# Delta stage of a four-stage sequence kernel: queries projected by channel and convolved on GpSimd, decay exponents read from rows in DRAM, beta as a bias of the exponential

## The reference

```
qkvz = x @ W_in                       # 128 -> 4*1024
q, k, v, z = split(qkvz)
b, a = split(x @ W_ba)                # 16 each
q, k, v = silu(conv(q, k, v))         # causal, 4 taps, one filter per channel
beta = sigmoid(b);  g = -exp(max(A_log, -2.3)) * softplus(a + dt_bias)
q = l2norm(q) * 64 ** -0.5;  k = l2norm(k)
for each position t:                  # S is 64x64 for each head
    S = S * exp(g[t])
    S = S + outer(k[t], (v[t] - k[t] @ S) * beta[t])
    o[t] = q[t] @ S
y = rmsnorm(o) * norm_w * silu(z)
out = y @ W_o
```

## Time and profile before

| | us |
|---|---|
| median of 3 runs | 7614.07 |
| lowest and highest | 7606.62 and 7653.81 |
| the profiled execution, its own time | 7602.55 |
| span of its trace | 7600.8 |

### The profile page before, as it was taken

One profiled execution on the slowest core, in us unless ns is written; L12 is line 12 of the kernel. 1 busy time (PEld: TensorE's weight loads), 2 busy tenths in 40 slices (PEclk: granted clock), 3 DMA queues, 4 the chain that ended last, 5 costly groups with the idle time before them and its releaser, 6 DMA issues. The chain is left out here.

```text
span 7600.8 us, 186089 instructions
## 1 busy us (share of the span) xinstructions
PE 6383.9 (84%) x68255; PEld 4549.0 (60%) x68256; DVE 3882.0 (51%) x7259; ACT 3145.8 (41%) x6176; POOL 1951.7 (26%) x1826
## 2 busy tenths in 40 slices
PE   2889999998999999999999999967588868887577
PEld 2566666666666666666666666646366646665477
DVE  3445545555455554555555555455444446666433
ACT  0444444444444444444444444414233325554155
POOL 2323223232232322223223232234100010001554
PEclk8999999999999999999999999979799989998588
DMA  3910000000000000000000000011100000000114
GB/s 101 322 35 1 2 1 1 1 1 2 1 1 2 1 2 1 1 1 1 2 1 1 2 1 1 1 35 50 33 0 0 0 2 0 0 0 22 36 56 117
DMA packets 92899, 160.08 MB, mean 21 GB/s; under 512 B 14156, under 2 KB 75636, under 8 KB 89588
## 3 DMA queue, kind: packets, MB, share of 16 engines
q1 hardware_dynamic: 70036, 121.89, 5.4%
q0 software_dynamic: 14080, 26.64, 1.0%
q10 hardware_dynamic: 8320, 4.19, 0.2%
HBM read 119.30 MB, written 104.06 MB: 29 GB/s over the span
## 5 line engine op out<-in xcount | busy, mean ns | idle before, releaser
L677 PE MATMUL bank<-wc,hT 128*128 128x512 f32 x3144 | 1517.6, 607 | 89.3 <-issue 83.9
L677 PEld LDWEIGHTS bank<-wc,hT 128*128 128x128 f32 x3144 | 557.8, 190 | 576.5 <-issue 560.8
L816 PE MATMUL bank<-X,kqe 128*128 128x64 f32 x6240 | 774.2, 277 | 74.9 <-DVE rb L1253 54.3
L816 PEld LDWEIGHTS bank<-X,kqe 128*128 128x128 f32 x6240 | 726.3, 192 | 98.9 <-DVE rb L1253 69.9
L1230 DVE TENSOR_TENSOR kqe<-bank,ex 128x512 f32<-128x512 f32 x520 | 335.1, 686 | 760.6 <-PE bank L723 760.6
L1285 DVE TENSOR_TENSOR yb<-bank,masks 128x512 bf16<-128x512 f32 x768 | 525.9, 685 | 234.9 <-PE bank L779 234.9
L1018 ACT ACTIVATE TT<-bank 128x512 bf16<-128x512 f32 x640 | 382.3, 597 | 539.0 <-PE bank L797 536.6
L1018 ACT ACTIVATE ex<-bank 128x512 bf16<-128x512 f32 x640 | 346.8, 594 | 392.4 <-PE bank L790 392.4
L949 ACT ACTIVATE th<-bank 128x512 f32<-128x512 f32 x523 | 304.7, 597 | 425.5 <-PE bank L677 409.0
L779 PEld LDWEIGHTS bank<-ex,mTb 128*128 128x128 bf16 x6144 | 253.7, 99 | 321.6 <-ACT ex L1018 185.7
L1125 POOL TENSOR_SCALAR_AFFINE_SELECT kqe<-kqe 128x512 f32<-128x512 f32 x260 | 215.7, 830 | 786.5 <-DVE kqe L1230 786.5
(11 more groups left out here) (511 smaller groups left out, 12883.3 us busy)
## 6 DMA issues: line engine op xcount, KB each, us to landing
sent_l0f<-blank_l0f SPq DMA_DIRECT2D x8, 4224.0 KB, 62.9
sent_l1m<-blank_l1m SPq DMA_DIRECT2D x8, 4224.0 KB, 134.7
xin<-sent_l1m SPq DMA_DIRECT2D x139, 66.0 KB
taken_l1m<-back_l1m SPq DMA_DIRECT2D x16, 512.0 KB, 8.7
cw_stage<-in_L_attn_conv_w_dram SPq DMA_DIRECT2D x6, 1024.0 KB, 5.5
xin<-sent_l0f SPq DMA_DIRECT2D x75, 66.0 KB
out_dram<-x_sb ACTq DMA_DIRECT2D x8, 512.0 KB, 7.4
back_l1m<-y,xin POOLq DMA_INDIRECT x136
```

Source lines behind the costliest of these rows:

```text
L677: mm = pe.matmul(bk[:, :], src[:, j:j + P], w["wc"][:, j, at * 512:(at + 1) * 512], start=(j == 0), stop=(j == TAPS - 1))
L816: mm = pe.matmul(bk[:, i * D0:(i + 1) * D0], lhsT(hh), rhs(hh), start=True, stop=True)
```

## The change

It is all in the delta stage.

- **Queries by channel.** `query_chunks` projects q once for each 128 channels (8 f32 matmuls, 131 columns: the tile and the three positions ahead of it) with unweighted `wq`. ScalarE copies the banks to `qp` (`query_rows`). GpSimd does the convolution in `convolve`: eight products with a tap broadcast along the row and six sums, 128x512 each. ScalarE's `tanh_q`, VectorE's `silu_q`, ScalarE's `squares_q` and TensorE's `query_squares` (8 f32 matmuls with the two columns of `pick`) follow in the level part. There is no turning of q: ScalarE copies `qa` to `kqT` in the decayed part.
- **Decay rows.** `delta_gates` also makes running sums of g, turns them and writes them as three bf16 parts to a DRAM tensor, `decay_rows`. Per tile, SyncE loads four pieces of 3x512 into `sums`, two tiles ahead. `decay` is then a bf16 matmul with 3 rows of ones and the same hiding matmul. `decay_rhs` is gone.
- **Beta in the bias.** log(beta) less the running sum is added as the bias of the exponential, by head: four activations of 128x128 in place of one of 128x512. `weigh_k`, `kbeta` and its turning are gone, and `products` takes the turned keys on both sides.
- **Roots.** The root of q's sum of squares is folded into `norm_o`: each of GpSimd's two powers per tile has 16 columns.
- `fill_blanks` is moved to ScalarE's queue, ahead of all its other work in `delta_attention`. `ex` and `T` no longer share memory. `delta_weights` does keys and values alone.

```diff
+            for i in range(nh):
+                pe.matmul(tb[i][:, :, :].rearrange("p k n -> p (k n)")[:, 0:half], mid[:, :],
+                          g_all[:, i * half:(i + 1) * half], start=True, stop=True).then_inc(turned_sums, 1)
...
-            fill_blanks(sp, sendings)
+            start_signals(sp, *rows_in)
+            def load(tile, t):
+                for hb in range(NHB):
+                    sp.dma_start(sums[32 * hb:32 * hb + 3, t, :].rearrange("c (o n) -> c o n", o=1),
+                                 decay_rows[:, tile, hb * HB:(hb + 1) * HB, :].rearrange("c o h n -> c o (h n)")
+                                 ).then_inc(rows_in[t].sem, 16)
...
+            def query_squares(b, f):
+                pe.wait_ge(sq_q.sem, sq_q.at(b, f + 1))
+                bk = dveb.fill(pe, b, "sq")
+                for pr in range(PAIRS):
+                    mm = pe.matmul(bk[:, 2 * pr:2 * pr + 2], sqT[:, pr, :], pick[:, :], start=True, stop=True)
...
         @block.scalar
         def _(act):
+            fill_blanks(act, sendings)
...
+                    for i in range(HB):
+                        ins = nc.scalar.activation(ex[:, hb % 2, i, :], bk[:, i * P:(i + 1) * P], ACT.Exp,
+                                                   bias=gates["bias"][:, f, hb * HB + i])
...
+                        if l == 3:
+                            tanh_q(b, t + 1)
...
+                for n, j in enumerate((TAPS - 1, *range(TAPS - 1))):
+                    for half, H in enumerate(halves):
+                        tap = w["cq"][:, H, j:j + 1].to_broadcast([P, 4, P])
+                        ins = pool.tensor_tensor((qt if n else qa)[:, H, :], qp[:, H, j:j + P], tap, ALU.mult)
...
+                    if n:
+                        for half, H in enumerate(halves):
+                            ins = pool.tensor_tensor(qa[:, H, :], qa[:, H, :], qt[:, H, :], ALU.add)
...
+                    convolve(b, t + 1)
+                    rsqrt_k(b, t + 1)
                     lone_wait(pool, proj.full.sem, proj.full.at(b, proj.uses.at(t, "z1")), pool_passed)
```

More of the change, by code:

```diff
@@ L270, in delta_weights, with delta_gates @@
     return sync, vector
[L273 removed]
+def delta_gates(nc, c, w, x_all, mr, gates, decay_rows, tiles):
     per = 4
@@ L312, in _ @@
             sp.wait_ge(loads, 32)
+            sp.wait_ge(pstep, 6)
+            sp.wait_ge(dstep, 9 + nh + 4 * nh)
+            for i in range(3):
+                sp.dma_start(decay_rows[i, 0:tiles, :, :].rearrange("(k t) h n -> (t h) k n", t=P // H0),
+                             three[:, i, :].rearrange("p (k n) -> p k n", n=P)).then_inc(kept, 16)
+                sp.dma_start(decay_rows[i, tiles:, :, :].rearrange("t h n -> (t h) n"), none[:, :]).then_inc(kept, 16)
+            sp.wait_ge(kept, 6 * 16)
         @block.gpsimd
@@ L354, in _ @@
                           start=True, stop=True).then_inc(sums, 1)
+            for i in range(nh):
+                pe.wait_ge(dstep, 10 + i)
+                for k in range(half // P):
+                    mm = pe.transpose(bb[i][:, k * P:(k + 1) * P], G[:, i * half + k * P:i * half + (k + 1) * P],
+                                      c["ident"][:, :])
+                mm.then_inc(turned_sums, 1)
         @block.scalar
@@ L656, in tail, with rows_of @@
             return t + 2
+        def rows_of(b, t):
+            return rows_in[(t + 1) % TPB].sem, rows_in[(t + 1) % TPB].at(b, 16 * NHB * (2 if t == 1 else 1))
         @block.sync
         def _(sp):
-            fill_blanks(sp, sendings)
+            start_signals(sp, *rows_in)
[4 more added lines that the diff above has]
+                                 ).then_inc(rows_in[t].sem, 16)
+            for t in range(TPB):
+                load(slice(t, t + 1), t)
+            with sp.Fori(0, turns) as b:
+                for t in range(TPB):
+                    lone_wait(sp, actb.full.sem, actb.full.at(b, actb.uses.at(t - 1, "ex.3")), sp_passed)
+                    load(bass.ds(b * TPB + t + TPB, 1), t)
+            for t in range(TPB):
+                sp.wait_ge(rows_in[t].sem, 16 * NHB * (turns + 2))
         @block.tensor
@@ L680, in taps, with query_chunks @@
                     mm.then_inc(proj.full.sem, 1)
+            def query_chunks(b, src, i):
+                bk = actb.fill(pe, b, f"qp.{i}")
+                for two in range(2):
+                    ch = 2 * i + two
+                    mm = pe.matmul(bk[:, two * 256:two * 256 + TAPS - 1 + P], w["wq"][:, ch * P:(ch + 1) * P], src[:, :],
+                                   start=True, stop=True)
+                mm.then_inc(actb.full.sem, 1)
+            def query_squares(b, f):
[3 more added lines that the diff above has]
+                    mm = pe.matmul(bk[:, 2 * pr:2 * pr + 2], sqT[:, pr, :], pick[:, :], start=True, stop=True)
+                mm.then_inc(dveb.full.sem, 1)
             def gate_tap(b, ch):
@@ L1260, in correct @@
                 ins.then_inc(dveb.done.sem, 1)
+            for a in range(2):
+                for half in range(2):
+                    dve.memset(pick[half * D0:(half + 1) * D0, a:a + 1], float(a == half))
             norm_h(0, 0, False)
```

394 lines of the change are left out of this document (232 added, 162 removed).

## The result

The changed kernel takes 7105.45 us (median of 4 runs, 7100.42 to 7113.03) where the one before takes 7610.34 (4 runs): ratio 0.934, 95% interval 0.932 to 0.936. The forecast was 7160 with a range from 7040 to 7330. The profiled run took 7100.42 us, with a span of 7098.7, 502.1 less than the span before.

The account below looks back on a forecast made before the run. TensorE was taken to bound the loop, its decayed part one for one. 7602.55 less 557 for 32 turns, plus 107 for ScalarE's held queue and 6 for set-up, gave 7158, stated as 7160 us; range 7040 to 7330.

Parts of the forecast that it names:

- the squares' 1.78: TensorE, level part: the eight two-column matmuls for q's sums of squares add 1.78 us per tile.
- 2 x 0.8 of new waits: Loop: new waits through ScalarE, VectorE and the products' banks take back 0.8 us per tile, twice a turn.
- the 19.0 of the sum: Loop: saving per two-tile turn from removed TensorE work and vanished waits, 19.0 us before new waits are subtracted.
- the sum's 7158: Whole kernel: profiled time 7602.55, less 557 in the loop, plus 107 and 6 ahead of it, 7158 us.
- The hold of ScalarE: Ahead of the loop: 18 blank DMAs hold ScalarE's queue before its first activation, everything 107 us later, bounds 0 to 110.
- the smaller set-up terms: Ahead of the loop: weights, gates, first tile's chain and decayed part, and table loads, together about +6 us.
- The cover that these issues had: Ahead of the loop: SyncE's slow issuing of blanks hurt nobody; on ScalarE the whole stage stands behind them.
- The verdict, covered: GpSimd, level part: the convolution takes 18.9 us of 27.2 available before ScalarE's tanh, 8 us to spare.
- The first (issues return at once): Ahead of the loop: ScalarE's queue is not held by the blank DMAs; 7060 us, chance 0.13.
- The second (clock behind the two-column matmuls): TensorE: clock falls once more per tile, losing 1 to 2 us; 7225 to 7350, middle 7290, chance 0.13.
- The third: GpSimd's convolution becomes the bound at ScalarE's tanh of q, from 27 us; slower than before at 34, chance 0.04.
- The last, half the gain: Matmuls of 3 rows or 131 columns cost full ones, or exponentials overlap nothing; 7440 us, chance 0.04.

Follow-up runs that it names:

- experiment 4: Changed kernel with a 512-column f32 matmul added per decay group: 7460.12 us; separately, with one 16-column matmul for the eight of the squares: 7085.31 us.
- experiment 6: Changed kernel with one exponential of 512 columns per group for four biased ones, leaving out decays and beta: 7121.29 us, ratio 0.937.
- experiment 2: Kernel before with only the 18 blank DMAs moved to ScalarE, ahead of its first activation: 7707.70 us, ratio 1.013.
- experiment 1: Changed kernel with the 18 blank DMAs issued by SyncE again, behind the first eight row loads: 7082.72 us, ratio 0.930.
- the third experiment: Changed kernel with blanks on SyncE in small lots, nine behind the first row loads and three after turns 4, 8 and 12: 7034.15 us, ratio 0.924.
- point 6: No run of its own: a reading of the granted clock over the loop, 1500 to 3500 us, in the traces of the kernel before, the changed one and variants.
- experiment 5: Changed kernel with the convolution's first pair of products repeated: 4 times more, 7107.21 us, ratio 0.935; 8 times more, 8066.06 us, ratio 1.061.

## Why the prediction was right, and by what

**The bound and the saved work.** Right. The decayed part of t = 0 was to be near 19.5 us and is 19.37; experiment 4 shows the one for one. Of the sizes, the squares' 1.78 are 1.80, eight chunks 2 x 0.98 = 1.96 for 1.78. The 3-row matmul, taken at the hiding matmul's 0.21, is 0.32 from start to start, 0.4 us more per tile.

**The saving per turn.** The turn was to be 17.4 us shorter and is 18.25 shorter. The mis-sized term is "2 x 0.8 of new waits": by the start-to-start times of one turn in each trace the parts are +0.27 (level part of t = 0), -9.86, +0.91 (of t = 1) and -10.40, -19.1 in all, just the 19.0 of the sum ahead of those waits. None of them came but for 0.39 for z: the exponentials are hidden (experiment 6), the products' groups follow one another without a gap, and the square of q is done in time. What took 0.9 of the 19.1 is what the sum has no term for, the clock's loss over many turns, 3.3 us a turn against 2.4. Two errors of opposite sign left the number near. With the first turn and the tail of the loop, 590 us were saved for 557. In all the profiled execution took 58 us less than the sum's 7158: 33 by the loop, 10 by what is ahead of it, and 15 behind it, which the sum had at nothing and which is luck, since variants of the kernel differ there by up to 39 us.

**The hold of ScalarE.** Right, and measured alone by experiment 2. The first activation comes 124.0 us after the first issue, against 10.4, so 113.6 in place of 107: the rest is that the issues took 122.8 and not 117.5. What I gave to the smaller set-up terms was +6 and came to -10.4: the first issue is 3.3 us later where I had 9, with the weights and gates together; from the first activation to the first level zero it is 49.7 us, not 63.4. I had -3 for the tables, the first chain and its decayed part. Ahead of the loop +103 for +113.

**What the hold rests on** I had half. "The cover that these issues had (SyncE had nothing else to do)" is true of before, and no longer of after: experiment 1 shows that SyncE now has row loads to issue, and that 70.7 MB of blanks in one queue delay them until TensorE waits 62 us. The call could not simply stay where it was. Of what was tried, only small lots keep both free.

**GpSimd.** The verdict, covered, was right and its margin too small. Products 1.03 for 1.04; sums 1.25 for 1.6. The row that I halved, 3.19 for the product of z, was itself lengthened by VectorE: VectorE's product of the roots and k, with two inputs in SBUF, ran beside it, and the same product of z with no such neighbour takes 2.35. I had used that contention to explain kbeta and not seen it in the other's row. So the convolution takes 16.5 us for 18.9, and has 9.5 and 12 us to spare for 8.

**The rivals.** The first (issues return at once) is refuted by the 105.30 us. The second (clock behind the two-column matmuls) is not refuted. The sign I had named, a clock of 1.00 behind them, holds in the turn shown and fails in others: the clock fell there in 5 of 31 tiles, at 10 us, 0.3 per tile for the 1 to 2 that I had given. In the third experiment it fell in 13 of 32, at 1.0 per tile. With bf16 or with one square it never did (point 6). So its mechanism is real and its frequency was too high; as much and more is lost at the reads of the state. The third did not occur, and experiment 5 confirms its mechanism and shows its price too low by half: I counted the wait and not the clock behind it. The last, half the gain, found nothing for it.

**Left open:** why the clock falls behind the squares and at the reads of the state in some turns and not in others, with the same work on TensorE; and the 15 us behind the loop by which the profiled run was quicker, of which 11 lie in the shared expert's stretch, at a clock of 0.93 for 0.86, in code that the change does not touch.

## What to carry to other kernels

Ask of a block of DMAs not only which engine issues it but what stands behind it twice: on the issuing engine, once some nine are on their way, and in the queue itself; small lots at places where nothing is due free both. Price a wait of TensorE of some microseconds with what follows it at half the clock, and fill a short wait with short work that is ready. Look at many turns, not at one, before saying that the clock does not fall in a place. When a duration is read off a row to price another engine's work, look first at what the neighbour did in that moment.

## What the runs showed of the hardware

- After eight blanks of 4224 KB and one of 726 KB had been issued at 0.6 to 0.7 us each, the next eight of 4224 KB took 105.30 us on ScalarE (after) and 99.33 on SyncE (first experiment), 13.2 and 12.4 on average, though single ones from 0.6 to 38.4. At the 304 to 319 GB/s of that time one transfer is 14 us.
- A small load on another queue moved within 15 us while the blanks held the DMA engines at 98%; behind them in one queue it came when they had ended (point 1).
- The normalised h of the next tile, a VectorE instruction with one tensor and two columns of scalars, takes 0.34 us before and 0.93 where GpSimd's sum runs beside it:

```profile
2075.19 0.93 DVE L1310 TENSOR_SCALAR x_sb<-x_sb,mr 128x128 f32 x1
```

It ends at 2076.12, just behind the sum's end at 2076.03. The reduction of 1024 columns beside the next sum takes its usual 1.21. The Trainium skill (SBUF — State Buffer, § Who interferes with whom) says that some one-input instructions such as this can take the shared port pair, and that a reduction never does on this chip; both agree with the rows.
- A wait of 5.10 or 8.21 us of TensorE was followed by 16 us and more at 0.50 either time, with TensorE busy throughout. A fall behind eight f32 matmuls of two columns came while TensorE was busy, and in some turns only.
- Eight f32 matmuls with two columns take 1.80 us, eight bf16 ones 0.35.
